# Decoder layer, expert stage: the second batch's router moved a round ahead, and another order of ScalarE's work

## The reference

```
x = LN(x + self_attention(x))               # 16 heads of 16, causal
x = LN(x + cross(slots = x, P = ctx))       # 3 rounds of softmax over slots, then a GRU cell
x = LN(x + experts(x))
# experts:
p    = sigmoid(x @ expert_sel.T)             # 16 experts
sel  = top 4 of p, divided by their sum, times route_scale
hid  = relu(x @ keys[e])                     # 64 wide for each expert
out  = sum over the 4 chosen e of sel[e] * (hid[e] @ values[e])
```

## Time and profile before

| | |
|---|---|
| median of 3 runs | 785.48 us |
| profiled execution | 783.54 us, of it 781.8 us from first to last instruction |
| TensorE busy | 670.6 us (86%), 5256 matmuls |
| VectorE busy | 476.0 us (61%) |
| ScalarE busy | 319.3 us (41%) |
| GpSimd busy | 231.9 us (30%) |
| mean granted TensorE clock | 0.934 |
| expert stage, from the first "gb" | 639.3 us to the end |

### The profile page before, as it was taken

The page is one execution under the profiler, slowest core; times in us unless marked ns, Lnnn a source line. Parts: engine busy times, 40 slices in busy tenths (PEclk is TensorE's granted clock), DMA queues, the critical chain, the costliest instruction groups (busy, mean ns, idle before and its releaser), DMA issues. The chain is left out here.

```text
span 781.8 us, 14311 instructions
## 1 busy us (share of the span) xinstructions
PE 670.6 (86%) x5256; PEld 615.3 (79%) x5256; DVE 476.0 (61%) x1013; ACT 319.3 (41%) x704; POOL 231.9 (30%) x257
## 2 busy tenths in 40 slices
PE   5567889989977999988999899998889894989986
PEld 4445668767766899888989889998888784978876
DVE  3444465647744667676667656767767765565543
ACT  3224445535752345434444424543344433243340
POOL 8112334324542332222231212212232313242332
PEclk9789998989998999999999789999999996989898
DMA  7766445354200400000000000000000000000000
GB/s 240 220 169 202 102 153 159 102 199 125 68 1 1 135 1 1 15 14 0 0 0 27 0 0 0 0 0 1 0 2 2 1 1 1 28 1 28 0 27 28
DMA packets 25679, 40.11 MB, mean 51 GB/s; under 512 B 2336, under 2 KB 11424, under 8 KB 25632
## 3 DMA queue, kind: packets, MB, share of 16 engines
q1 hardware_dynamic: 25632, 39.49, 16.5%
HBM read 24.67 MB, written 14.68 MB: 50 GB/s over the span
## 5 line engine op out<-in xcount | busy, mean ns | idle before, releaser
L1122 DVE TENSOR_REDUCE neg_max<-bank 128x2 f32<-128x512 f32 (+1 forms) x96 | 65.4, 690 | 83.7 <-PE bank L1614 56.3
L398 PE MATMUL bank<-slots_hl,whhT_hl 128*128 128x256 f32 x864 | 112.2, 289 | 0.3 <-PEq L1821 0.3
L1895 PE MATMUL bank<-attn_hl,vg_hl 128*128 128x256 f32 x864 | 109.3, 286 | 1.3 <-ACT attn_hl L715 1.1
L398 PEld LDWEIGHTS bank<-slots_hl,whhT_hl 128*128 128x128 f32 x864 | 107.4, 194 | 1.7 <-issue 0.6
L1895 PEld LDWEIGHTS bank<-attn_hl,vg_hl 128*128 128x128 f32 x864 | 104.9, 194 | 1.7 <-ACT attn_hl L715 1.4
L751 ACT ACTIVATE pT<-bank 128x512 f32<-128x512 f32 x96 | 56.9, 598 | 68.0 <-PE bank L1627 52.2
L597 POOL TENSOR_SCALAR_AFFINE_SELECT pT<-pT 128x512 f32<-128x512 f32 x64 | 40.8, 641 | 120.4 <-ACT pT L751 120.4
L678 POOL TENSOR_TENSOR slots_hl<-slots,slots_hl 128x512 fp32r<-128x512 f32 x16 | 20.4, 1277 | 137.0 <-ACT slots_hl L715 137.0
L701 POOL TENSOR_TENSOR hid_hl<-hid,hid_hl 128x512 fp32r<-128x512 f32 x32 | 40.8, 1286 | 56.5 <-ACT hid_hl L715 56.3
L398 PE MATMUL bank<-x2T_hl,keys_hl 128*128 128x256 f32 x384 | 54.0, 298 | 0.0
L398 PEld LDWEIGHTS bank<-x2T_hl,keys_hl 128*128 128x128 f32 x384 | 51.3, 204 | 0.2
(11 more groups left out here) (189 smaller groups left out, 1370.3 us busy)
## 6 DMA issues: line engine op xcount, KB each, us to landing
q_rows<-q_hl SPq DMA_DIRECT2D x24, 256.0 KB
k_rows<-k_hl SPq DMA_DIRECT2D x24, 256.0 KB
q_op<-q_rows SPq DMA_DIRECT2D x32, 192.0 KB, 3.3
k_op<-k_rows SPq DMA_DIRECT2D x16, 384.0 KB, 5.5
xT_in<-in_xT_dram SPq DMA_DIRECT2D x4, 512.0 KB, 4.3
x_in<-in_x_dram SPq DMA_DIRECT2D x8, 256.0 KB, 5.7
c_in<-in_ctx_dram SPq DMA_DIRECT2D x8, 256.0 KB, 3.1
out_dram<-y_out SPq DMA_DIRECT2D x8, 256.0 KB, 2.1
```

The costliest lines, as they stand in the source:

```text
L398: mm = pe.matmul(dst, left(a), right(b), start=first and n == 0, stop=last and n == 2, skip_group_check=True)
L1122: dve.tensor_reduce(dst, src, AX.X, ALU.max, negate=True).then_inc(max_ok, 1)
L1895: mm = pe.matmul(halves(b)[:, m, :], vg_hl[:, j, v_part, 3 * t + r, q:q + P], attn_hl[:, j, at_part, t, :], start=n == 2 and a + m + t == ...
```

## The change

In rounds 0 to 2, "lT" of batch 1 for the next round becomes TensorE's job behind "o 1"; exp follows it on ScalarE, and `route` on VectorE between the moments and the normalization of batch 1's output. "gT 1" then stands as third job of the next round, `gates_hi` first on ScalarE and `gates_lo` behind `gated(0)`. "tT 0" and "lg 0" move a few jobs back. ScalarE's `relu(n + 4)` now stands ahead of `hidden_hi(n + 1)`, and `expert_text_hi(i + 1, 0, 0)` behind `hidden_hi(4)`. In round 0 batch 1's router stays in the round, ahead of the two `last_norm`, which now stand behind `gated(3)` and `gated(4)`; GpSimd does their powers behind lo(3) and lo(4). ScalarE's round 0 is now written out apart.

```
-EXPERT_ORDER = [gb0, gb1, lT1, h4, gb2, h5, gb3, h6, gT1, tT0, gb4, h7, gb5, lg0, gb6, gb7, tT1,
-                half0, lT0, o0, lg1, half1, gT0, o1, h0, h1, h2, h3]
+EXPERT_ORDER = [gb0, gb1, gT1, h4, gb2, h5, gb3, h6, gb4, h7, tT0, gb5, gb6, gb7, lg0, tT1,
+                half0, lT0, o0, lg1, half1, gT0, o1, lT1, h0, h1, h2, h3]      # AHEAD gains lT1
 GpSimd
-    if first and n < 2: rstd(PAIRS - 1, var2, rstd2, std2, n + 1, n)
+    if first and n in (3, 4): rstd(PAIRS - 1, var2, rstd2, std2, n - 2, n - 3)
 ScalarE, text(): in round 0
-    act.wait_ge(x2_ok, due(2, PAIRS - 1, 2))
+    act.wait_ge(uT_mm, due(2, PAIRS - 1, 2))
 ScalarE, experts()
-    hidden_hi(0); exp_logits(i, 1, 1)
-    hidden_hi(1); relu(i, 4)
-    text(i + 1, 0)
-    hidden_hi(2); relu(i, 5)
-    text(i + 1, 1)
-    hidden_hi(3); relu(i, 6); gates_hi(i, 1, 1)
-    expert_text_hi(i + 1, 0, 0)
-    hidden_hi(4); relu(i, 7)
+    hidden_hi(0); exp_logits(0, 1, 1)         # first
+    gates_hi(i, 1, 1); hidden_hi(0)           # else
+    relu(i, 4); hidden_hi(1)
+    text(i + 1, 0)
+    relu(i, 5); hidden_hi(2)
+    text(i + 1, 1)
+    relu(i, 6)
+    gates_hi(0, 1, 1)                         # first
+    hidden_hi(3); relu(i, 7); hidden_hi(4)
+    expert_text_hi(i + 1, 0, 0)
     hidden_hi(5); hidden_hi(6); hidden_hi(7)
     expert_text_hi(i + 1, 1, 1); exp_logits(i + 1, 0, 0); gates_hi(i + 1, 0, 0)
+    exp_logits(i + 1, 1, 1)
     relu(i + 1, 0 to 3)
 VectorE, experts()
-    gated(0); gated(1); gated(2); last_norm(0) if first; route(i, i, 1)
-    gated(3); last_norm(1) if first; gates_lo(i, 1, 1)
-    expert_text_lo(i + 1, 0, 0)
-    gated(4); gated(5); logits(i + 1, 0, 0); gated(6); gated(7)
+    gated(0); gates_lo(i, 1, 1) if not first
+    gated(1); route(0, 0, 1) if first
+    gated(2); gates_lo(0, 1, 1) if first
+    gated(3); last_norm(0) if first
+    gated(4); last_norm(1) if first
+    expert_text_lo(i + 1, 0, 0)
+    gated(5); gated(6); gated(7); logits(i + 1, 0, 0)
 VectorE, output of batch j
-    layer_norm(...)
+    moments(...)
+    if j and not last: route(i, i + 1, 1)
+    normal(...)
 TensorE, round 0: turned_logits(0, 1, 1) ahead of h4, turned_gates(0, 1, 1) ahead of gb4
```

More of the change, by code:

```diff
@@ L367, in context_bank @@
             return FIRST_BANK[key][0] if first else BANK2[key]
-        EXPERT_ORDER = [("gb", 0), ("gb", 1), ("lT", 1), ("h", 4), ("gb", 2), ("h", 5), ("gb", 3), ("h", 6), ("gT", 1), ("tT", 0),
[2 rows of a table removed]
+        EXPERT_ORDER = [("gb", 0), ("gb", 1), ("gT", 1), ("h", 4), ("gb", 2), ("h", 5), ("gb", 3), ("h", 6),
[2 rows of a table added]
                         ("h", 0), ("h", 1), ("h", 2), ("h", 3)]
-        AHEAD = (("tT", 0), ("tT", 1), ("lg", 0), ("lT", 0), ("lg", 1), ("gT", 0), ("h", 0), ("h", 1), ("h", 2), ("h", 3))
+        AHEAD = (("tT", 0), ("tT", 1), ("lg", 0), ("lT", 0), ("lg", 1), ("gT", 0), ("lT", 1), ("h", 0), ("h", 1), ("h", 2), ("h", 3))
         FIRST_TEXT = (1, 3)
@@ L702, in experts @@
                                            f32(hid_hl[:, j, HI, 2 * g:2 * g + 2, :]), ALU.subtract).then_inc(h_lo, 1)
-                        if first and n < 2:
-                            rstd(PAIRS - 1, var2, rstd2, std2, n + 1, n)
+                        if first and n in (3, 4):
+                            rstd(PAIRS - 1, var2, rstd2, std2, n - 2, n - 3)
                 for j in range(2):
@@ L1002, in _, with text @@
             cross(PAIRS - 1, last=True)
-            def text(i, j):
-                act.wait_ge(x2_ok, due(2, PAIRS - 1, 2))
+            def text(i, j, first=False):
+                if first:
+                    act.wait_ge(uT_mm, due(2, PAIRS - 1, 2))
+                else:
+                    act.wait_ge(x2_ok, due(2, PAIRS - 1, 2))
                 act.wait_ge(tT_mm, due(2, i, j + 1, back=1))
@@ L1030, in relu, with experts @@
                 act.activation(hid[:, n % 4, :, :], halves(4 + n % 2), ACT.Relu).then_inc(h_relu, 1)
-            def experts(i, last):
+            def experts(i, last, first=False):
                 def hidden_hi(n):
@@ L1037, in hidden_hi @@
                     copy(hid_hl[:, j, HI, 2 * g:2 * g + 2, :], hid[:, g, :, :]).then_inc(h_hi, 1)
-                hidden_hi(0)
-                exp_logits(i, 1, 1)
+                if first:
+                    hidden_hi(0)
+                    exp_logits(0, 1, 1)
+                else:
+                    gates_hi(i, 1, 1)
+                    hidden_hi(0)
+                relu(i, 4)
                 hidden_hi(1)
-                relu(i, 4)
                 if not last:
-                    text(i + 1, 0)
+                    text(i + 1, 0, first)
+                relu(i, 5)
                 hidden_hi(2)
-                relu(i, 5)
                 if not last:
-                    text(i + 1, 1)
+                    text(i + 1, 1, first)
+                relu(i, 6)
+                if first:
+                    gates_hi(0, 1, 1)
                 hidden_hi(3)
-                relu(i, 6)
-                gates_hi(i, 1, 1)
+                relu(i, 7)
+                hidden_hi(4)
                 if not last:
                     expert_text_hi(i + 1, 0, 0)
-                hidden_hi(4)
-                relu(i, 7)
                 hidden_hi(5)
@@ L1068, in _ @@
             gates_hi(0, 0, FIRST_TEXT[0])
-            with act.Fori(0, PAIRS - 1) as i:
+            experts(0, False, True)
+            with act.Fori(1, PAIRS - 1) as i:
                 experts(i, False)
@@ L1530, in experts @@
             def experts(i, last, first=False):
-                links[0] = EXPERT_LINKS_BEFORE
+                links[0] = EXPERT_LINKS_BEFORE * (1 if first else 2)
                 def gated(n):
@@ L1537, in experts @@
                 gated(0)
+                if not first:
+                    gates_lo(i, 1, 1)
                 gated(1)
+                if first:
+                    route(0, 0, 1)
                 gated(2)
                 if first:
-                    last_norm(0)
-                route(i, i, 1)
+                    gates_lo(0, 1, 1)
                 gated(3)
                 if first:
+                    last_norm(0)
+                gated(4)
+                if first:
                     last_norm(1)
-                gates_lo(i, 1, 1)
                 if not last:
                     expert_text_lo(i + 1, 0, 0)
-                for n in range(4, 6):
+                for n in range(5, 8):
                     gated(n)
@@ L1552, in experts @@
                     logits(i + 1, 0, 0)
-                gated(6)
-                gated(7)
-                if not last:
                     expert_text_lo(i + 1, 1, 1)
@@ L1566, in experts @@
                     dve.wait_ge(stored[j], due(1, i, 1, back=1, step=16))
-                    layer_norm(i, expert_chain, EXPERT_LINKS, lambda t: u3[:, t, :], stats3, mv3, std3, var3, rstd3, j + 1,
-                               lambda t: y_out[:, j, t, :], y_ok)
-                assert last or links[0] == EXPERT_LINKS_BEFORE + EXPERT_LINKS
+                    moments(i, expert_chain, EXPERT_LINKS, lambda t: u3[:, t, :], stats3, mv3, std3, var3)
+                    if j and not last:
+                        route(i, i + 1, 1)
+                    normal(i, lambda t: u3[:, t, :], mv3, std3, rstd3, j + 1, lambda t: y_out[:, j, t, :], y_ok)
+                assert last or links[0] == 2 * EXPERT_LINKS_BEFORE + EXPERT_LINKS
             experts(0, False, True)
@@ L1959, in experts @@
                     ahead = (name, n) in AHEAD
-                    if ahead and last:
+                    if ahead and last or first and (name, n) == ("gT", 1):
                         continue
+                    if first and (name, n) == ("h", 4):
+                        turned_logits(0, 1, 1)
+                    if first and (name, n) == ("gb", 4):
+                        pe.wait_ge(lx_ok, due(2, 0, 2))
+                        turned_gates(0, 1, 1)
                     if first and (name, n) in (("tT", 0), ("half", 0)):
```

## The result

The changed kernel takes 789.38 us, the median of 19 runs, against 784.5 us of the kernel before in 19 runs beside it: a ratio of 1.0061, 95% interval 1.004 to 1.0081, so 3 to 6 us slower. The profiled execution is one of 786.80 us, with a span of 785.1 us.

A forecast was written before the change was run, and what follows sets the result against it. TensorE's idling for the router and its time at the lower clock were taken as the bound. Round 0 +1.4, loop rounds +5.0, last round -1.6 make +4.8 us: 785.48 becomes 790.3, range 785.2 to 794.5.

The forecast's parts named there:

- The pitch: Rounds 1 and 2: with the relu ahead of the next high part, one turn from tile to tile takes 2.60 us.
- The chain to "gb 7": Rounds 1 and 2: four turns, text high and low parts, then `gated(5)`; "gb 7" 14.6 us behind "gb 0".
- H: Start of `hidden_hi(0)` in a round, from which the prediction counts; forecast 1.62 us behind "gb 0" in rounds 1 and 2.
- The pause and the clock: Rounds 1 and 2: TensorE idles about 5 us before "gb 7", lower clock costs 2.2 us; +2.5 us a round.
- Rival (b): Rounds: the pause comes but the clock hardly suffers; 783.5 to 786 us, no change; chance 12%.
- (c): Rounds: slow clock twice in a round, or `route` meets GpSimd's power; +1.5 to +2 more per loop round, 794 us; 10%.
- Round 0: Round 0: late gates and normalizations behind low parts delay TensorE, "half 0" at H + 22.6; +1.4 us with "lT 1".
- The last round: Last round: no text in the way, "half 0" 11.5 us behind "gb 0"; -1.6 us, between gains of 2.1 and 0.9.
- The shared ports: `route` against GpSimd's power for the output: if the power starts first, the sum is 2 us higher; not added.
- Rival (a): Rounds: the router's wait goes and nothing replaces it, if the pitch is below about 2.0 us; 772 us; chance 7%.

The follow-up runs named there:

- e1: The changed kernel with `hidden_hi(n + 1)` ahead of `relu(n + 4)` again for tiles 1 to 4 in rounds 1 to 3; ratio to the kernel before 0.9883.
- e2: The kernel before with only `relu(n + 4)` put ahead of `hidden_hi(n + 1)`, tiles 1 to 3, all rounds; ratio to the kernel before 1.0027.
- e4: The changed kernel with 32 extra matmuls in TensorE's pause ahead of "gb 7" in rounds 1 and 2; ratio to the kernel before 0.9981.
- e7: e1 with, in round 0, the high parts ahead of the relus and `gates_hi` right behind `hidden_hi(2)`; ratio to the kernel before 0.9873.
- e3: The changed kernel with `expert_text_hi(i + 1, 0, 0)` between `hidden_hi(3)` and `relu(7)` in rounds 1 and 2; ratio to the kernel before 0.9939.
- e5: e1 with round 0 put back as in the kernel before on all four engines; ratio to the kernel before 0.9886.

## Why the prediction was right

The forecast was 790.3 us, +4.8; the medians have +4.9 and the rounds of the two traces +3.8. The mechanism came as told. That the medians agree to a tenth is chance: their interval goes from 3 to 6 us, and the last round gained 0.8 us more than forecast. The absolute forecast also started from 785.48, where the kernel before has a median of 784.5 over 19 runs.

- **The pitch.** 2.60 us a turn was forecast. The relus of tiles 4 and 5 stand at 721.72 and 724.30, 2.58 apart, and `relu(7)` at 729.42, 7.70 behind the first: 2.57 a turn. e1 shows that this order is the cause of the long rounds, e2 that it is one only together with the router's move.
- **The chain to "gb 7".** Forecast 14.6 us behind "gb 0", measured 14.08. The half microsecond lies mostly in H: 1.31 instead of 1.62, the rest in the turns behind it. One sign named in the prediction did not come: `gated(0)` starts 0.51 us behind "gb 0", as in the kernel before, and not 0.8. VectorE in round 2 of the changed kernel, normalization and `gated(0)`:

```profile
717.58 0.73 DVE L1346 TENSOR_SCALAR y_out<-u,mv,std 128x256 f32<-128x256 f32 x2
718.82 0.69 DVE L1546 TENSOR_TENSOR hid<-bank,hid 128x512 f32<-128x512 f32 x1 [0.51 <-PE bank L2004]
```

VectorE is free at 718.31, when "gb 0" starts, 0.76 us earlier against it than forecast. 0.46 of this is the add, taken as 0.68 us behind "h 0", which with "lT 1" in front would be 0.46; it began together with "h 0" (712.45). The row chosen was the latest of three: in the trace of the kernel before the add stands 0.20, 0.68 and 0.44 us behind "h 0" (675.47, 710.12, 744.14). Why it varies is open. So `route` in front of the normalization did not delay the chain.

- **The pause and the clock.** 5 us were forecast and 4.83 recorded. The clock's loss was sized at 2.2 us a round; e4 gives 2.2 and 2.75. So a loop round was forecast at +2.5 and measured at +2.25 and +2.67. In round 2 two misses cancel: the chain half a microsecond shorter, the clock's loss half a microsecond larger. The prediction lets the clock of the earlier trace rows fall "while TensorE waited"; it fell at 723.20, just behind the start of "gT 1" at 722.95, between the two waits. Rival (b), a clock that hardly matters, is out by e4. Of (c) neither part came: "h 7" ran at full speed, with a single slow stretch of 6.80 us in round 2, and `route` began before the power.
- **Round 0.** Forecast +1.4, measured +1.32. "half 0" starts 22.6 us behind H, as worked out (640.10 and 662.70 in the trace), but by luck. "gb 4" came at H + 9.9 instead of 9.3 and "gb 7" at H + 20.0 instead of 19.7; the way from there to "half 0" then took 2.6 us instead of 2.9. The gates behind `relu(6)` are the larger part of the delay (2.0 us in e7). The prediction names no second meeting of `route` with a low part; it cost 0.9 us.
- **The last round.** The mechanism was right and the size too small: -2.44 instead of -1.6. "half 0" starts 11.09 us behind "gb 0" where 11.5 was forecast, and the clock did not fall, which I had half counted:

```profile
766.33 5.89 PE L398 MATMUL bank<-values_hl,hid_hl 128*128 128x256 f32 x48 [1.23 <-POOL hid_hl L701]
772.66 5.89 PE L398 MATMUL bank<-values_hl,hid_hl 128*128 128x256 f32 x48 [0.44 <-POOL hid_hl L701]
```

- **The shared ports.** `route`'s first instruction in its new place and the power for the output, in round 1 of the changed kernel:

```profile
677.91 0.17 DVE L1363 TENSOR_SCALAR prb<-prb 128x32 f32<-128x32 f32 x1
678.08 0.69 POOL L581 TENSOR_TENSOR std<-std,half_neg 128x2 f32<-128x2 f32 x1 [4.86 <-DVE std L1336]
```

It starts before the power and takes 0.17 us, so the 2 us were rightly left out; what the other order would have cost, no run shows. In round 0, `route` meets the low parts, and there not its first instruction alone:

```profile
640.85 1.29 DVE L1363 TENSOR_SCALAR prb<-prb 128x32 f32<-128x32 f32 x1 [0.19 <-ACT prb L1018]
643.64 1.09 DVE L1381 TENSOR_TENSOR gate<-prb,prbx 128x32 f32<-128x32 f32 x1
```

The second, with two operands in SBUF, took 0.19 us in the loop; lo(1) ran from 643.39 to 644.69. The Trainium skill ("SBUF — State Buffer", Who interferes with whom) names two SBUF inputs as the other case in which VectorE and GpSimd contend, and the trace agrees.

Rival (a) asked for a pitch below 2.0 us; e1 brings lo(0) to lo(3) to (727.70 - 723.06) / 3 = 1.55 us, and the round falls to 30.6 us, 3.6 to 3.7 under the kernel before. But the pitch alone does not decide: e3 keeps 2.58 us and its loop rounds are still 0.9 us shorter than before. What decides is when the text and, behind it, `gated(5)` are let go.

## What to carry to other kernels

Moving a wait away from a busy engine gains only what the next chain leaves; follow each helper engine's queue in its written order, tile by tile, and compare its pitch with the slowest single step in it (here 2.58 us against 1.28). Then see which job behind that chain is the one the busy engine waits for: e3 moved only that job and won half of the pause back. On an engine that works in order, an instruction that waits for another engine's answer must not stand ahead of the one that the other engine needs next: `relu(n + 4)` waited for GpSimd, which waited for the high part queued behind that relu. Price a pause on TensorE twice, once for its length and once for the clock behind it.

## What the runs showed of the hardware

- A pause of TensorE cost 2.2 and 2.75 us a round on top of its own length, by the clock alone (e4). Whether a pause of 2.15 us lowers the clock differed between rounds of the same code: in e1 it didn't, in round 1 of e5 it did, at 1.6 us.
- An instruction of VectorE on 128x32 elements with two operands in SBUF took 0.19 us alone and 1.09 us beside a low part of GpSimd (round 0 of the changed kernel); in e7, with the low parts over, 0.19 us again.
- The instructions ahead of the expert stage are the same in all ten kernels, and its first "gb" still stood anywhere between 638.78 us (changed kernel) and 647.50 us (e1) in the profiled executions. That spread is larger than the change; only the rounds inside one trace, or many runs, tell such kernels apart.
